# Normalized tiles and heads transposed by DMA, the first slab of keys used by four head pairs, the queries of block 1 computed within block 0

## The chip, the cores and the metric

The kernel runs as one program on the 8 cores of one Trainium2 chip. Each core works on its own data and exchanges nothing with the others. The metric is the device time of the slowest core in microseconds (us), one launch of the kernel; a time is the median of several runs. The kernel before takes 1018.23 us (three runs, 1016.39 to 1018.49).

## The reference

One transformer layer in float32, over x of shape (4, 4096, 1024): multi-query attention (16 heads of 64, one key and one value head) and a small per-channel network, both behind a layer norm and with a residual.

```python
r = layernorm(x)                                   # over the last axis, eps 1e-5
q = einsum('bnd,hkd->bnhk', r, query_proj)         # 16 heads of 64
k = einsum('bmd,dk->bmk', r, key_proj)             # one key head
v = einsum('bmd,dv->bmv', r, value_proj)           # one value head
attn = softmax(einsum('bnhk,bmk->bnhm', q, k) / 8)
o = einsum('bnhm,bmv->bnhv', attn, v)
x = x + einsum('bnhv,dhv->bnd', o, output_proj)
r = layernorm(x)
s = r @ Win + bin_                                 # (b, t, 64)
g = einsum('btmh,mh->btm', relu(s[..., None] * W1 + b1), W2) + b2
x = x + g @ Wout + bout
```

## The kernel before

Two cores share a batch entry: each owns 2048 of its 4096 rows as queries and needs the keys and values of all 4096. A core therefore normalizes 32 tiles of 128 rows (`NTILES`), its own 16 first, then the 16 of its neighbour. Four tiles are a slab of 512 rows, so there are 8 slabs (`NSLAB`).

**The main loop.** The queries are taken in 4 blocks of 512 (`NK`), the 16 heads in 8 pairs (`NHP`). One step of the loop, called an exp below, is one pair, one block of queries and one chunk of 128 keys: TensorE makes the scores of both heads, two matmuls of 512 columns (L662), into one of two PSUM buffers (`spa`, `spb`); ScalarE takes the exponential of 128x1024 values and writes bf16 (`ptu`, L816); TensorE multiplies them with the values in 8 matmuls of 65 columns (L457), the 65th column giving the softmax's sum. There are 4 x 8 x 32 = 1024 of them, numbered 0 to 1023. TensorE issues the scores of exp g+2 when exp g is done, so ScalarE has at most two ahead of it. Each engine works through its instructions in order.

**Segments.** `SEGS` lists in which order pairs and key chunks go. Blocks 1 to 3 take a pair through all 32 chunks, then the next pair. Block 0 has to start before all keys exist: pairs 0 and 1 take slab 0 (exps 0 to 7), then both take slab 1 (exps 8 to 15), pairs 2 to 7 take slabs 0 and 1 (to exp 63), and then each of the slabs 2 to 7 goes through all pairs, 32 exps each, the partial sums being added up in `oacc` (`o_out`, L725). So slab 1 is wanted from exp 8, slab 2 from exp 64, slab 3 from exp 96, slab 7 from exp 224.

**Side work.** All else on TensorE is a list of uses (`USES`) that go in turn through two further PSUM banks, `sda` and `sdb`; VectorE empties each (one `sev` count per use, waited for by `wait_ev`). In block 0 (`phase_a_order`) a slab takes four uses `tr` (a normalized tile `r1u` of 128x1024 transposed in 8 matmuls against the identity, L372, and copied out into `r1t` by VectorE, L504), one `K` (8 matmuls of 512 columns, L380) and one `V` (32 of 64 columns, L391). `Q` makes the queries of one pair, 8 matmuls (L402). Of a finished pair the head outputs `on` are transposed in the use `ot` (4 matmuls, L410, copy L517) into `ot`. In blocks 1 to 3 (`later_order`) the output projection of the block before (`op`, two uses a tile), the transposed normalized output tile (`rt`), the small network (`s2`, 23 VectorE operations, `fo`) and queries of a later block are woven in. VectorE also does the layer norm: two `bn_stats` and an aggregation (L468 to L471), then, when GpSimd has made the reciprocal deviation (L836, L838), the normalization (L478).

**The planner.** `pace` runs through the exps in order, without times: when a use is wanted it forces all that stands before it, and otherwise it hands out one piece of TensorE's side work and one of VectorE's an exp. Its counts fix where in each engine's program a piece stands.

**DMA.** SyncE's queue (SP) loads the tiles of x: the first four at once, tiles 4 to 7 into `xtra`, each of the others when the buffer it takes is free (L883, it waits for a normalized tile). GpSimd's queue (POOL) loads the weights, which are converted from float32 to bf16 on the way: `wqb` in eight parts (L854), and `winb`, `woutb` and the output projection `wp`, behind tile 20's deviation (L857 to L860).

The first slab is built by a stretch of its own at the program's start, and the last two output tiles in a tail behind the last exp.

## Time and profile before

| | |
|---|---|
| median of 3 runs | 1018.23 us |
| profiled execution | 1017.6 us |
| its span on the slowest core (core 4) | 1016.1 us (all cores 1012.9 to 1016.1) |
| ScalarE busy | 952.2 us, 94% |
| TensorE busy | 900.6 us, 89% |
| VectorE busy | 358.7 us, 35% |
| chain that ended last | ScalarE's exponential 80% of the span, issue 9%, PE 5%, VectorE 3%, DMA 3% |
| first exp starts, last exp starts | 24.18 us, 984.56 us |

The span runs from the first to the last instruction of a core; the execution's own time is 1.5 us longer. Busy time is the union of an engine's instructions, and exps overlap each other by some 0.3 us, so an exp's own duration is longer than the step from one to the next. A time with "idle before" in a row is what the engine stood still in front of that instruction, and the name behind the arrow is what it then got.

### The profile page before, as it was taken

How to read it: one execution, taken by the hardware profiler on the slowest of the kernel's cores; microseconds unless marked ns; L12 is line 12 of the kernel's file. 1: busy time of each engine (PE TensorE's matmuls, PEld its weight loads, DVE VectorE, ACT ScalarE, POOL GpSimd, SP SyncE). 2: the span in 40 equal slices, each digit the busy share in tenths (PEclk: the TensorE clock that was granted, in tenths of full speed). 3: DMA queues.
4: the chain of work that ended last, by engine and by line, in shares of the span. 5: the costliest groups of instructions: out<-in, count | busy, mean ns of one | idle time of the engine just before them, and what ended most of it. 6: DMA issues, size and time to landing. Idle time of an engine off the chain costs nothing.

```text
span 1016.1 us, 28595 instructions; the slowest of 8 cores (1012.9 to 1016.1 us)
## 1 busy us (share of the span) xinstructions
PE 900.6 (89%) x11582; PEld 493.1 (49%) x11712; DVE 358.7 (35%) x637; ACT 952.2 (94%) x1043; POOL 56.5 (6%) x131
## 2 busy tenths in 40 slices
PE   3898899998899999998889999998889998898884
PEld 3445555555444545544444454544444554454442
DVE  4535666652512222234202122244202326424215
ACT  2597999999999999999999999999999999999981
POOL 3201111100000000000000000000000000000000
PEclk9999999999999999999999999999999999999995
DMA  8502257220000000002200000001210000400101
GB/s 196 138 12 85 85 119 174 85 85 3 1 2 2 2 2 2 2 2 84 85 2 2 1 3 1 2 2 62 58 51 2 2 2 2 167 2 1 44 2 41
DMA packets 13406, 40.94 MB, mean 40 GB/s; under 512 B 3168, under 2 KB 3296, under 8 KB 13152
## 3 DMA queue, kind: packets, MB, share of 16 engines
q1 hardware_dynamic: 8208, 26.26, 8.5%
q0 software_dynamic: 4784, 12.32, 5.3%
q8 instruction: 97, 1.59, 0.7%
q10 hardware_dynamic: 288, 0.52, 0.1%
q14 instruction: 29, 0.24, 0.1%
HBM read 35.70 MB, written 8.39 MB: 43 GB/s over the span
## 4 chain that ended last, share of the span: by engine, by line
ACT 80%; issue 9%; PE 5%; DVE 3%; DMA 3%; POOL 0%; DVEq 0%; SPq 0%; POOLq 0%; ACTq 0%
ACT ptu L816 80%; DMA xtra<-x_own 2%; PE ob L457 1%; DMA xbuf<-x_own 1%; PE spa L662 1%; PE spb L662 1%; DVE r1u L478 1%; PE sda L380 0%; DVE r1t L504 0%; DVE lnst L468 0%; PE spb L695 0%; DVE lnst L469 0%; DVE gacc L787 0%; POOL rstd L838 0%; PE sdb L391 0%
## 5 line engine op out<-in xcount | busy, mean ns | idle before, releaser
L816 ACT ACTIVATE ptu<-spa 128x1024 bf16<-128x1024 f32 x512 | 594.5, 1161 | 17.7 <-PE spa L662 17.6
L816 ACT ACTIVATE ptu<-spb 128x1024 bf16<-128x1024 f32 x512 | 595.9, 1164 | 2.9 <-PE spb L662 2.9
L457 PE MATMUL ob<-vab,ptu 128*128 128x65 bf16 x8192 | 409.1, 195 | 0.7 <-ACT ptu L816 0.5
L457 PEld LDWEIGHTS ob<-vab,ptu 128*128 128x128 bf16 x8192 | 298.4, 97 | 208.4 <-issue 208.4
L662 PE MATMUL spb<-qt,k2t 64*128 64x512 bf16 x1024 | 200.8, 380 | 40.5 <-ACT ptu L816 34.9
L662 PE MATMUL spa<-qt,k2t 64*128 64x512 bf16 x1024 | 200.9, 380 | 36.5 <-ACT ptu L816 28.3
L662 PEld LDWEIGHTS spb<-qt,k2t 64*128 64x128 bf16 x1024 | 63.4, 92 | 127.2 <-issue 108.1
L662 PEld LDWEIGHTS spa<-qt,k2t 64*128 64x128 bf16 x1024 | 62.6, 92 | 114.5 <-issue 95.1
L725 DVE TENSOR_TENSOR oacc<-oacc,ob 128x520 f32<-128x520 f32 x50 | 34.8, 696 | 77.3 <-PE ob L457 77.2
L836 POOL TENSOR_SCALAR lnve<-lnmv 128x1 f32<-128x1 f32 x48 | 12.7, 264 | 658.0 <-DVE lnmv L471 658.0
L527 DVE TENSOR_TENSOR xbuf<-xbuf,sda 128x512 f32<-128x512 f32 x16 | 11.0, 688 | 93.3 <-PE sda L423 80.0
L527 DVE TENSOR_TENSOR xbuf<-xbuf,sdb 128x512 f32<-128x512 f32 x16 | 11.0, 688 | 89.5 <-PE sdb L423 54.9
L732 DVE RECIPROCAL zrec<-ob 128x8 f32<-128x8 f32 x24 | 5.0, 207 | 100.1 <-PE ob L457 99.8
L478 DVE TENSOR_SCALAR r1u<-xbuf,lnmv,rstd 128x1024 bf16<-128x1024 f32 x44 | 35.6, 810 | 9.1 <-POOL rstd L838 9.1
L423 PE MATMUL sda<-xtra,ot 128*128 128x512 bf16 x98 | 37.0, 379 | 0.0
L402 PE MATMUL sdb<-r1t,wqb 128*128 128x512 bf16 x104 | 35.9, 380 | 0.1
L423 PE MATMUL sdb<-xtra,ot 128*128 128x512 bf16 x96 | 35.4, 379 | 0.2 <-issue 0.2
L513 DVE CAST qt<-sdb 128x512 bf16<-128x512 f32 x16 | 11.0, 690 | 69.5 <-PE sdb L402 40.8
L402 PE MATMUL sda<-r1t,wqb 128*128 128x512 bf16 x96 | 34.4, 380 | 0.1
L468 DVE BATCH_NORM_STATS2 lnst<-xbuf 128x6 f32<-128x512 f32 x44 | 30.3, 689 | 10.9 <-DMA xbuf<-x_own 7.7
L513 DVE CAST qt<-sda 128x512 bf16<-128x512 f32 x15 | 10.3, 690 | 61.4 <-PE sda L402 42.9
L469 DVE BATCH_NORM_STATS2 lnst<-xbuf 128x6 f32<-128x512 f32 x44 | 29.7, 676 | 0.0
(123 smaller groups left out, 471.1 us busy)
## 6 DMA issues: line engine op xcount, KB each, us to landing
xbuf<-x_own SPq DMA_DIRECT2D x28, 512.0 KB, 4.4
xbuf<-x_oth SPq DMA_DIRECT2D x16, 512.0 KB, 3.9
out<-xbuf POOLq DMA_DIRECT2D x14, 512.0 KB, 3.6
wqb<-wq POOLq DMA_DIRECT2D x8, 256.0 KB, 9.6
xtra<-x_own SPq DMA_DIRECT2D x4, 512.0 KB, 6.9
xtra<-wp POOLq DMA_DIRECT2D x1, 2048.0 KB, 21.0
boutbc_s<-boutbc SPq DMA_DIRECT2D x1, 512.0 KB, 12.7
out<-xbuf SPq DMA_DIRECT2D x2, 256.0 KB, 2.6
```

The lines of the kernel that those rows point to most:

```text
L402: r = te.matmul(bank[:], wqb[:, b, j, :], r1t[:, a, j, :], start=(j == 0), stop=(j == DCH - 1))
L423: r = te.matmul(bank[:], ot[:, blk % 2, c, t * 128:(t + 1) * 128], wpb[:, c, b * 512:(b + 1) * 512], start=(c == 0), stop=(c == heads - 1))
L457: r = te.matmul(osum[:, hd, c * 65:(c + 1) * 65], ptu[:, g % NPT, hd * 512 + c * 128:hd * 512 + (c + 1) * 128], vab[:, a + i, :], start=(i ...
L468: v.bn_stats(lnst[:, q, 0:6], xt(li)[:, 0:512])
L469: v.bn_stats(lnst[:, q, 6:12], xt(li)[:, 512:1024]).then_inc(bns, 1)
L478: v.tensor_scalar(r1u[:, li % 2, :], xt(li), lnmv[:, q, 0:1], rstd[:, q, :], op0=ALU.subtract, op1=ALU.mult).then_inc(nrm, 1)
L513: v.tensor_copy(qt[:, a % 2, b, :], bank[:]).then_inc(sev, 1)
L527: v.tensor_tensor(xh, xh, bank[:], op=ALU.add).then_inc(sev, 1)
L662: mm = te.matmul(sps[g % 2][:, hh * 512:(hh + 1) * 512], k2t[rows, mc * 128:(mc + 1) * 128], q, start=True, stop=True)
L725: v.tensor_tensor(oacc[:, hp], oacc[:, hp], osum, op=ALU.add).then_inc(oev, 1)
L816: sc.activation(ptu[:, g % NPT, :], sps[g % 2][:], AF.Exp, scale=0.125).then_inc(ex, 1)
L836: e.tensor_scalar(lnve[:, q, :], lnmv[:, q, 1:2], EPS, None, op0=ALU.add).then_inc(veps, 1)
```

## The change

- `SEGS`: pairs 0 to 3 take slab 0 (exps 0 to 15), then slab 1 (16 to 31); pairs 4 to 7 take both (to exp 63). Slabs 2 to 7 are wanted when they were.
- A normalized tile goes from `r1u` to `r1t` by one DMA transpose from SP's queue (`tile_transpose`), without TensorE, PSUM and VectorE. `r1u` has four buffers in place of two; the normalization of tile n waits for the transpose of tile n-4. The same holds for the output tiles (`rt`), except the last two, and for the heads (`head_transpose`, 31 of 32; in the last block two DMAs a pair). The uses `tr`, `rt` and all `ot` but the last are gone.
- `phase_a_order`: V of slab 0 now stands ahead of the first scores; queries of pairs 1 to 3 come before K of slab 1. The queries of block 1 all follow the last V in block 0; those of block k+1 are spread over block k.
- The planner has costs (in hundredths of a us: an exp 92, a matmul of side work 22), a lag that each engine may carry, and puts a transpose at 6 exps from the normalization (`TR_LAG`). It also writes down the order of the transposes for SP (`moves`).
- VectorE may normalize a whole slab ahead of its K (a table `AHEAD`), in block 0 about a tile every 4 exps, from tile 8 at exp 19 to tile 31 at exp 114.
- SP: a tile's transpose is preceded by the load of tile n+4. The transposes of slabs 5, 6 and 7 wait until V of the slab two before has left PSUM, because they take its buffer in `r1t`. Loads of the output tiles 4 to 15 go to POOL's queue. Parts of `wqb` are issued in another rhythm (two behind tile 3).

```diff
-SEGS = [(0, 0, 0, 4), (0, 1, 0, 4), (0, 0, 4, 8), (0, 1, 4, 8)]
-SEGS += [(0, hp, 0, 8) for hp in range(2, NHP)]
+SEGS = [(0, hp, 4 * sl, 4 * sl + 4) for sl in range(2) for hp in range(4)]
+SEGS += [(0, hp, 0, 8) for hp in range(4, NHP)]
...
 def phase_a_order():
-    o = [("V", 0, 0)] + q(0, 1) + slab(1) + [("V", 1, 0)]
-    o += q(0, 2, 3, 4, 5, 6, 7)
+    o = [("V", 0, 0)] + q(0, 1, 2, 3) + [("K", 1, 0), ("V", 1, 0)] + q(0, 4, 5, 6, 7)
     for s in range(2, NSLAB):
-        o += slab(s) + [("V", s, 0)]
-    return o + q(1, 0) + [("ot", 0, hp) for hp in range(NHP - 1)]
+        o += [("K", s, 0), ("V", s, 0)]
+    return o + q(1, *range(NHP))
...
+        pe_lag = min(pe_lag + PIECE * forced, PE_LAG)
+        t = SCORES + HALF * len(halves) + (SWITCH if halves or forced else 0)
+        while head["pe"] is not None and ok(head["pe"], 1):
+            if pe_lag + t + switch + PIECE - SLOT > PE_LAG:
+                break
+            run("pe", pe, "pe")
...
-        r1u = sbuf("r1u", [128, 2, D], BF16)
+        r1u = sbuf("r1u", [128, 4, D], BF16)
...
                 elif kind == "K":
-                    yield [("sev", n)]
-                    wait_ev(te, n - 1)
+                    yield [free, ("trd", 4 * a + 4)]
+                    wait_ev(te, n - 2)
+                    for q in range(4):
+                        te.wait_ge(trl[q], 16 * a)
...
         def ln_norm(v, li):
             v.wait_ge(rsd, li + 1)
-            if 2 <= li < 6:
-                v.wait_ge(ptr, li - 1)
+            if 4 <= li < 8:
+                v.wait_ge(ptr, li - 3)
+            elif li >= 8:
+                v.wait_ge(trl[q], 16 * (li // 4 - 1))
...
-                if 2 <= i <= NHP:
-                    e.dma_start(wqb[:, i - 1], ...).then_inc(wql[i - 1], 16)
+                for c in {2: [1], 3: [2, 3], 5: [4], 6: [5], 7: [6], 8: [7]}.get(i, []):
+                    e.dma_start(wqb[:, c], ...).then_inc(wql[c], 16)
...
+        def tile_transpose(e, li, dst):
+            e.wait_ge(nrm, li + 1)
+            e.dma_start_transpose(dst, r1u[:, li % 4, :]).then_inc(trl[li % 4], 16)
+
+        def head_transpose(e, k, i):
+            n = 8 * k + i
+            if i == 0 and k >= 2:
+                wait_ev(e, USE_NO["op", 4 * (k - 2) + 3, 1])
+            e.wait_ge(onr, n + 1)
+            if k < LAST:
+                e.dma_start_transpose(ot[:, k % 2, i, :]..., on[:, n % 2]...).then_inc(otl[n % 2], 16)
...
+            for kind, n in moves:
...
+                sl = n // 4
+                if n >= 8:
+                    e.wait_ge(nrm, n + 1)
+                    src = xtile(n + 4) if n < NTILES - 4 else xo_r[n % 4]
+                    e.dma_start(xbuf[:, n % 4, :], src).then_inc(xl[n % 4], 16)
+                if sl in (5, 6, 7) and n % 4 == 0:
+                    last = [i for i, u in enumerate(USES) if u[:2] == ("V", sl - 2) or sl == 5 and u[:2] == ("Q", 0)]
+                    wait_ev(e, max(last))
+                tile_transpose(e, n, r1t[:, slab_buf(sl), :, n % 4 * 128:n % 4 * 128 + 128])
...
+                if n == 20:
                     e.dma_start(boutbc[:], bout_d).then_inc(boutl, 16)
```

In the lists below a row is an instruction, or several alike (x8), with its line, what it writes and what it reads. TensorE before, from the first scores to the scores of exp 8 (L662 scores, L457 values, L391 V, L402 Q, L372 a tile's transpose, L380 K):

```order
L662 MATMUL spa<-qt,k2t 128x512 x2
L662 MATMUL spb<-qt,k2t 128x512 x2
L662 MATMUL spa<-qt,k2t 128x512 x2
L391 MATMUL sda<-wvb,r1t 128x64 x32
L402 MATMUL sdb<-r1t,wqb 128x512 x8
L662 MATMUL spb<-qt,k2t 128x512 x2
L457 MATMUL ob<-vab,ptu 128x65 x12
L372 MATMUL sda<-identb,r1u 128x128 x8
L662 MATMUL spa<-qt,k2t 128x512 x2
```

And TensorE with the change, from the same point (L706 scores, L498 values, L426 V, L438 Q):

```order
L426 MATMUL sda<-wvb,r1t 128x64 x32
L706 MATMUL spa<-qt,k2t 128x512 x2
L706 MATMUL spb<-qt,k2t 128x512 x2
L706 MATMUL spa<-qt,k2t 128x512 x2
L438 MATMUL sdb<-r1t,wqb 128x512 x3
L706 MATMUL spb<-qt,k2t 128x512 x2
L498 MATMUL ob<-vab,ptu 128x65 x12
L438 MATMUL sdb<-r1t,wqb 128x512 x5
L706 MATMUL spa<-qt,k2t 128x512 x2
```

V of slab 0 has moved in front of the first scores, and the eight matmuls of Q stand on both sides of the scores of exp 3. Q of pairs 2 and 3 follow in the same way before exps 8 and 12. K of slab 1 stands directly in front of the scores of exp 16, with no exp's work among its matmuls:

```order
L706 MATMUL spa<-qt,k2t 128x512 x2
L706 MATMUL spb<-qt,k2t 128x512 x2
L498 MATMUL ob<-vab,ptu 128x65 x12
L415 MATMUL sda<-r1t,wkb 128x512 x8
L706 MATMUL spa<-qt,k2t 128x512 x2
```

The later slabs' K stand spread over 5 to 8 exps: K of slab 2 begins behind the values of exp 45, that of slab 3 behind 59, of slab 4 behind 74, of slab 5 behind 92, of slab 6 behind 110 and of slab 7 behind 121. VectorE empties V of slab 3 among the work of exp 81, V of slab 4 at exp 100 and V of slab 5 at exp 113.

VectorE before, from tile 5's normalization to K of slab 1 (L478 normalization, L504 a transposed tile out of PSUM, L508 K out of PSUM):

```order
L478 TENSOR_SCALAR r1u<-xtra,lnmv,rstd 128x1024
L504 COPY r1t<-sda 128x8x128
L478 TENSOR_SCALAR r1u<-xtra,lnmv,rstd 128x1024
L504 COPY r1t<-sdb 128x8x128
L478 TENSOR_SCALAR r1u<-xtra,lnmv,rstd 128x1024
L504 COPY r1t<-sda 128x8x128
L504 COPY r1t<-sdb 128x8x128
L508 CAST k2t<-sda 128x512
```

VectorE with the change, behind the second emptying of `ob`, around tiles 6 to 8 (L509 to L515 statistics, L528 normalization, L562 Q out of PSUM):

```order
L528 TENSOR_SCALAR r1u<-xtra,lnmv,rstd 128x1024
L509 BN_STATS lnst<-xbuf 128x6
L513 BN_STATS lnst<-xbuf 128x6
L515 BN_AGGR lnmv<-lnst 128x2
L528 TENSOR_SCALAR r1u<-xtra,lnmv,rstd 128x1024
L562 CAST qt<-sdb 128x512
```

The first row normalizes tile 6, the statistics are those of tile 8, the next normalization is tile 7's, and Q of pair 3 is emptied behind it.

SP's queue with the change, tiles 20 to 23 (the third row's wait for `sem_side_evac` is the one for V of slab 3):

```order
L971 DMA xbuf<-x_oth 128x1024 [waits sem_normed]
L926 DMA_TRANSPOSE r1t<-r1u 128x8x128 [waits sem_side_evac,sem_normed]
L983 DMA boutbc_s<-boutbc 128x1024
L971 DMA xbuf<-x_oth 128x1024 [waits sem_normed]
L926 DMA_TRANSPOSE r1t<-r1u 128x8x128 [waits sem_normed]
L971 DMA xbuf<-x_oth 128x1024 [waits sem_normed]
L926 DMA_TRANSPOSE r1t<-r1u 128x8x128 [waits sem_normed]
L971 DMA xbuf<-x_oth 128x1024 [waits sem_normed]
L926 DMA_TRANSPOSE r1t<-r1u 128x8x128 [waits sem_normed]
```

Before, SP's queue held loads alone there; now four transposes and four loads stand behind that one wait. Behind the waits of slabs 6 and 7 stand four transposes and three loads each. The load of `wp` follows tile 20's deviation as before, which is now due at about exp 64.

## Rows read from the trace of the kernel before

**Rows 1.** The page: busy time and span share of ScalarE's two groups.

```profile
L816 ACT ACTIVATE ptu<-spa 128x1024 bf16<-128x1024 f32 x512 | 594.5, 1161 | 17.7 <-PE spa L662 17.6
L816 ACT ACTIVATE ptu<-spb 128x1024 bf16<-128x1024 f32 x512 | 595.9, 1164 | 2.9 <-PE spb L662 2.9
```

**Rows 2.** Timeline of ScalarE: start, duration, then idle time before and releaser.

```profile
24.18 1.02 ACT L816 ACTIVATE ptu<-spa 128x1024 bf16<-128x1024 f32 x1 [0.32 <-PE spa L662]
28.93 1.02 ACT L816 ACTIVATE ptu<-spb 128x1024 bf16<-128x1024 f32 x1 [1.89 <-PE spb L662]
31.43 1.02 ACT L816 ACTIVATE ptu<-spa 128x1024 bf16<-128x1024 f32 x1 [1.48 <-PE spa L662]
41.78 1.02 ACT L816 ACTIVATE ptu<-spa 128x1024 bf16<-128x1024 f32 x1 [6.58 <-PE spa L662]
51.27 1.02 ACT L816 ACTIVATE ptu<-spa 128x1024 bf16<-128x1024 f32 x1 [2.06 <-PE spa L662]
101.67 1.02 ACT L816 ACTIVATE ptu<-spa 128x1024 bf16<-128x1024 f32 x1 [6.29 <-PE spa L662]
105.29 1.02 ACT L816 ACTIVATE ptu<-spb 128x1024 bf16<-128x1024 f32 x1 [0.77 <-PE spb L662]
...
969.89 1.20 ACT L816 ACTIVATE ptu<-spb 128x1024 bf16<-128x1024 f32 x1
970.81 1.20 ACT L816 ACTIVATE ptu<-spa 128x1024 bf16<-128x1024 f32 x1
...
984.56 1.20 ACT L816 ACTIVATE ptu<-spb 128x1024 bf16<-128x1024 f32 x1
```

**Rows 3.** Timeline of TensorE at the start and at K of slab 2.

```profile
23.70 0.39 PE L662 MATMUL spa<-qt,k2t 64*128 64x512 bf16 x2 [0.20 <-DVE qt L756]
25.68 1.11 PE L391 MATMUL sda<-wvb,r1t 128*128 128x64 bf16 x32
38.56 1.67 PE L380 MATMUL sda<-r1t,wkb 128*128 128x512 bf16 x7 [1.16 <-DVE r1t L504]
...
96.98 3.00 PE L380 MATMUL sda<-r1t,wkb 128*128 128x512 bf16 x7 [2.10 <-DVE r1t L504]
```

**Rows 4.** Timeline of VectorE: tile 7's statistics, a normalization, Q's emptying.

```profile
29.91 0.68 DVE L513 CAST qt<-sdb 128x512 bf16<-128x512 f32 x1
30.52 0.68 DVE L468 BATCH_NORM_STATS2 lnst<-xtra 128x6 f32<-128x512 f32 x1
31.12 0.68 DVE L469 BATCH_NORM_STATS2 lnst<-xtra 128x6 f32<-128x512 f32 x1
35.84 0.81 DVE L478 TENSOR_SCALAR r1u<-xtra,lnmv,rstd 128x1024 bf16<-128x1024 f32 x1
```

**Rows 5.** Stretches (24 to 52, 280 to 986): busy time by engine, PEclk, DMA.

```profile
24.00:52.00 28.00, 22.27 (x289) 12.73 (x289) 15.30 (x28) 15.81 (x17) 6.32 (x12) 1.00 0.58 137
280.00:986.00 706.00, 646.87 (x8279) 346.58 (x8385) 194.72 (x351) 705.00 (x768) 18.80 (x42) 1.00 0.07 21
```

**Rows 6.** DMA queue q1: 2.0 to 2.5 us, 105 to 107.2 us; last row q0, 7 to 10.5 us.

```profile
q1 hardware_dynamic: 128, 0.03, 26.4%
q1 hardware_dynamic: 144, 0.52, 72.9%
q0 software_dynamic: 703, 0.09, 39.9%
```

**Rows 7.** DMA issues: KB each, median us from issue to landing.

```profile
xbuf<-x_oth SPq DMA_DIRECT2D x16, 512.0 KB, 3.9
identb<-ident SPq DMA_DIRECT2D x1, 32.0 KB, 2.2
xtra<-wp POOLq DMA_DIRECT2D x1, 2048.0 KB, 21.0
```

**Rows 8.** DMA issues of 150 to 160 us, while `wp` is loaded.

```profile
xbuf<-x_oth SPq DMA_DIRECT2D x1, 512.0 KB, 10.8
```

274 lines of the change are left out of this document (154 added, 120 removed).

## Prediction

> **What bounds the kernel now.** I read the page's groups first, then ScalarE's timeline, then its stretches. The two exponential groups are all that counts: 1024 of them, each a step of 970.81 - 969.89 = 0.92 us (0.917 over a long row of them) [rows 1, 2]. From 280 to 986 us ScalarE is busy 705.0 of 706.0 us with 768 of them [rows 5]: nothing that TensorE or VectorE save there can shorten the time. The first starts at 24.18, the last at 984.56 [rows 2]. 1023 steps of 0.917 are 938.1, the stretch is 960.4, so 22.3 us at most can be won inside, and the page puts 17.7 + 2.9 = 20.6 us of idle time on TensorE's scores [rows 1]. The timeline names them: 1.89, 1.48, 6.58 and 2.06 before exp 16, then 6.29 and 0.77 at slab 2 [rows 2]; 19.1 of the 20.6. In front of the program stand 24 us, behind it a tail of 31 us that the change leaves alone. So the sum is made at five places, all in front of exp 130.
>
> **Part by part.**
>
> *V of slab 0 before the first scores.* V takes 1.11 us; the first scores stood at 23.70 behind Q's emptying, with 0.20 idle [rows 3]. I take 0.9 us later: the first exp at 25.1.
>
> *Exps 0 to 16.* Before, exp 16 started at 51.27, 12.4 us behind an unbroken row from 24.18 (38.85) [rows 2]. Slab 1 is now wanted at exp 16, not 8, but Q of pairs 1, 2 and 3 at exps 4, 8 and 12. Exp 4: Q's last matmul ends at about 29.2, but VectorE first has two tiles' statistics (four times 0.68 and two aggregations, 3.0) and a normalization (0.81) [rows 4], so Q leaves PSUM at 30.0 and exp 4 starts at 30.5, 1.7 behind a row from 25.1. Exp 8: Q's end 34.3, emptying 0.7 to 0.8, scores 0.5: 35.6, 1.4 lost. Exp 12: Q stands behind the statistics of tile 8 and the normalization of tile 7, which ends at 40.3: 41.3, 2.0 lost. Exp 16: K of slab 1 starts when the scores of exp 15 (behind exp 13, which ends at 43.3) and the values of exp 13 are done, 44.2; its eight matmuls are 8/7 of 1.67 = 1.9 [rows 3], the emptying 0.8, the scores 0.5: 47.4. That holds if tile 7's transpose, issued at 40.7, has landed by 44.2.
>
> *What a transpose by DMA costs.* No row shows one. A tile is 1024 pieces of 256 B. Nearest rows: 128 packets of 256 B (the identity) took 26.4% of 16 engines in 0.5 us, 16.5 ns each on one engine, so a tile is 1.06 us of all 16; the small packets of `wk` (128 B written) took 39.9% of 3.5 us for 703, 32 ns each, so 2.0 us [rows 6]. From issue to landing the identity took 2.2 us [rows 7]. Bounds for a tile alone: 2.2 and 4.2 us; behind a load of x that is under way, 1.6 us more (72.9% of 2.2 us) [rows 6]. I take 1.06 us of the queue and 3.3 to landing. The lower bound of what it can do to the time is nothing, since a landing before its K leaves no trace. Tile 7: 40.7 + 3.3 and part of a neighbour = 44 to 45, so I put exp 16 at 48.2: 3.1 us won against 51.27.
>
> *Slab 2.* Before, K of slab 2 waited for transposes and copies, ran at the lower clock (3.00 us against 1.67 for the same seven matmuls) and cost 6.29 + 0.77 [rows 2, 3]. Now tile 11 is normalized at exp 33 and K begins at 45: 12 x 0.917 = 11 us for a transpose of 3.3 behind one load (3.9 [rows 7]). 7.1 us won.
>
> *Smaller waits.* 20.6 - 19.1 = 1.5 us of idle time elsewhere. VectorE loses 28 + 14 copies of a tile, TensorE as many transposes: I take 1.0 won.
>
> *Slabs 5, 6, 7: the new wait.* Their transposes wait for V of the slab two before to leave PSUM, and K is placed soon behind: exps 81 to 92, 100 to 110, 113 to 121, that is 10.1, 9.2 and 7.3 us, and each about 0.5 more, since K follows the values. In that time q1 has to move four transposes (4 x 1.06) and four, three and three loads (1.6 each), and the last one's landing adds 2.3 (3.9 - 1.6) [rows 6, 7]: 12.9, 11.3 and 11.3 us. Late by 2.3, 1.6 and 3.5. ScalarE has up to two exps of scores in hand, worth 0.6 us after the next scores' own time: 1.7 + 1.0 + 2.9 = 5.6. Where TensorE waits for a `trl` count, the scores of the next exp stand behind it, and ScalarE waits for these. Ends: 0 (SP's own loads spread before the wait) and, with 2.0 us a transpose, 3.8 more in each, 17. I take 5.6, next to the identity's row.
>
> *Heads and output tiles in blocks 1 to 3.* The head DMA has half a tile; the output projection stands 7 exps (6.4 us) behind the pair's end, of which VectorE takes 2: 4.4 us for about 3. Nothing lost. If it were 4.2 + 1.6, 1.4 us less 0.6 in each of three blocks: 2.4. Loads of output tiles wait on POOL for the stores, far from their use. `r1u`'s wait for the transpose four tiles back stands on VectorE with `oacc`'s emptying behind it, but 16 exps behind it in time except at slabs 5 to 7, where it is the same lateness.
>
> Sum against the profiled execution: 1017.6 - 3.1 - 7.1 - 1.0 + 5.6 = 1012.0. The median of the runs is 0.6 above that execution: 1012.6, which I give as 1012.5.
>
> **The rivals.**
>
> *A, the forecast:* 1008 to 1016.
>
> *B, all of it hidden.* The loads behind the three waits are mostly done before, or transposes take less than their slots; then 1018.2 - 11.2 = 1007, down to 1003 if exps 4 to 16 also lose less (5.1 us are counted there). For: ScalarE has no other stops; against: four loads stand behind one wait in the order of SP's queue.
>
> *C, slower: the transposes of slab 5 behind the load of `wp`.* It is issued about exp 66 and needs 21.0 us, 23 exps, so to exp 89; a load of x issued in its middle took 10.8 us in place of 3.9 [rows 7, 8]. The four transposes and four loads of slab 5 start at exp 82 in the midst of it. The last 7 us of `wp` add up to 6.9; VectorE stops too, since tile 24's normalization waits for tile 20's transpose. Then slab 5 costs 1.7 + 6.9 = 8.6, and a load of tile 24 that comes late (stands before the statistics at exp 78) 1 to 2 more, and with 2.0 us a transpose the other slabs 3.8 each. 1018.2 - 11.2 + 8.6 + 3.9 + 1.5 = 1021, up to 1032; it decides from the point at which the waits sum to 11.2 us. I give 1023. For: the same queue and the 10.8. Against: packets of both queues do alternate, and K of slab 4 is placed before. The Trainium skill, "DMA: Bandwidth & Descriptors" ("Queues, rings and completion order"), says that an engine takes turns between its queues packet by packet; by that the 7 us of `wp` would cost slab 5 about half, 3.5, and C's 1021 would be an estimated 1018. The 10.8 beside 3.9 [rows 7, 8] speaks for more than half, since the measured load lost 6.9 us to some 9 of `wp`.
>
> *D, the start does not gain.* Tile 7's transpose stands behind the loads of tiles 8 to 11 and weights (58% DMA share from 24 to 52 us [rows 5]) and lands at 47 or later: exp 16 at 51, 1015.5 with the rest as in A, 1018 with part of C.
>
> *E, a transpose is far dearer.* If its eight blocks of 128x128 went one behind the other, each like the identity's 2.2 us [rows 7], a tile took 17.6 us, 28 tiles 493; the last would land at 30 + 493 = 523 us, wanted at exp 222, 229 us: some 290 us slower, 1310. The Trainium skill, "VectorE: DVE Perf Modes", speaks against the change: "Transpose 128×128: use TensorE if PSUM dest is OK" ("Rules for kernel authors"), with 1309 ns for one block by DMA ("The three transpose paths"). By that, in series, a tile would be 10.5 us and the time an estimated 1110; nothing in this trace shows it.
>
> **How the numbers follow.** Of no change this kernel's measurement can tell 0.2%, 2 us: 1016.2 to 1020.3 is "same". Chances: A 0.37, B 0.22, C 0.25, D 0.12, E 0.04. Faster: A, B and a quarter of D lie under 1016.2, less what of A spills over: 0.60. Same: three quarters of D and the lower edge of C: 0.13. Slower: the rest of C, and E: 0.27. The range leaves out E and the outer parts of B and C: 1003 to 1030; the forecast's own is 1008 to 1016.
>
> **What would show it.** First exp at 25 us; exp 16 at 47 to 49; no idle time at slab 2; waits of ScalarE's exponential at exps 93 to 97, 111 and 122, the first the longest if C holds, with TensorE waiting for a DMA `r1t<-r1u`. A DMA row of about 3.3 us for `r1t<-r1u`. From exp 130 on, no idle time, and a tail of 31 us. Wrong would be: transposes over 6 us to landing, stops in blocks 1 to 3 at the output projection, or an exp step above 0.917.

## The result, and the profile after

The changed kernel takes 1071.95 us (median of 4 runs, 1070.02 to 1106.12) against 1018.05 of the kernel before; the ratio is 1.0526, 95% interval 1.0498 to 1.0554. It is slower by 54 us, and the prediction of 1012.5 (1003 to 1030) was wrong.

The page of the changed kernel (slowest core: 5): queues, the two groups of exponentials (busy us, mean ns, then idle us before them and what ended most of it), K's matmuls, the first half of a tile's statistics, and two DMA issues (count, KB, median us to landing).

```profile
q1 hardware_dynamic: 67920, 35.06, 16.7%
q0 software_dynamic: 6512, 18.61, 6.8%
...
L864 ACT ACTIVATE ptu<-spa 128x1024 bf16<-128x1024 f32 x512 | 557.7, 1089 | 49.5 <-PE spa L706 48.0
L864 ACT ACTIVATE ptu<-spb 128x1024 bf16<-128x1024 f32 x512 | 557.8, 1089 | 16.3 <-PE spb L706 16.0
...
L415 PE MATMUL sda<-r1t,wkb 128*128 128x512 bf16 x56 | 22.6, 465 | 27.7 <-DMA r1t<-r1u 27.6
L509 DVE BATCH_NORM_STATS2 lnst<-xbuf 128x6 f32<-128x512 f32 x44 | 30.4, 690 | 37.0 <-DMA xbuf<-x_oth 27.9
...
xtra<-wp POOLq DMA_DIRECT2D x1, 2048.0 KB, 20.4
r1t<-r1u SPq DMA_TRANSPOSE x42, 5.2
```

ScalarE's idle time went from 17.7 + 2.9 [rows 1] to 49.5 + 16.3 us, and two new waits stand behind it: TensorE's K matmuls for the transposes of tiles, 27.6 us, and VectorE's statistics for loads of x, 27.9 us. A transpose of a tile took 5.2 us from issue to landing, in the median of all 42. ScalarE's timeline on the slowest core (start, duration, then idle time and releaser) shows where the time went:

```profile
23.67 1.02 ACT L864 ACTIVATE ptu<-spa 128x1024 bf16<-128x1024 f32 x1 [1.49 <-PE spa L706]
29.40 1.02 ACT L864 ACTIVATE ptu<-spa 128x1024 bf16<-128x1024 f32 x1 [1.96 <-PE spa L706]
34.95 1.02 ACT L864 ACTIVATE ptu<-spa 128x1024 bf16<-128x1024 f32 x1 [1.76 <-PE spa L706]
41.15 1.02 ACT L864 ACTIVATE ptu<-spa 128x1024 bf16<-128x1024 f32 x1 [2.41 <-PE spa L706]
61.20 1.02 ACT L864 ACTIVATE ptu<-spa 128x1024 bf16<-128x1024 f32 x1 [16.23 <-PE spa L706]
...
130.40 1.02 ACT L864 ACTIVATE ptu<-spb 128x1024 bf16<-128x1024 f32 x1 [11.15 <-PE spb L706]
149.79 1.02 ACT L864 ACTIVATE ptu<-spa 128x1024 bf16<-128x1024 f32 x1 [7.09 <-PE spa L706]
175.05 1.02 ACT L864 ACTIVATE ptu<-spa 128x1024 bf16<-128x1024 f32 x1 [6.05 <-PE spa L706]
198.84 1.02 ACT L864 ACTIVATE ptu<-spa 128x1024 bf16<-128x1024 f32 x1 [6.59 <-PE spa L706]
...
1037.79 1.09 ACT L864 ACTIVATE ptu<-spb 128x1024 bf16<-128x1024 f32 x1
```

These are exps 0, 4, 8, 12 and 16, then 77, 88, 108, 124 and the last, 1023; the last began at 984.56 before [rows 2]. Slab 2's 6.29 us have gone; 16.23 (K of slab 1), 11.15 (K of slab 4), 7.09, 6.05 (both `oacc`) and 6.59 us (K of slab 7) have come.

Why the transposes of slab 1 and tile 19 of slab 4 were late is in the queue that issues them, SP's (start, us that the issue took):

```profile
27.62 23.71 SPq L926 DMA_TRANSPOSE r1t<-r1u  x4
...
104.68 1.36 SPq L926 DMA_TRANSPOSE r1t<-r1u  x1
108.75 0.33 SPq L971 DMA_DIRECT2D xbuf<-x_oth  x1
109.17 10.52 SPq L926 DMA_TRANSPOSE r1t<-r1u  x1
119.78 5.23 SPq L971 DMA_DIRECT2D xbuf<-x_oth  x1
```

A single issue took 1.36 us behind one load of x (1.22 in the later blocks, where nothing stood beside it), about 6 in slab 1, beside parts of `wqb` and loads of x, and 10.52 beside the load of `wp`. So SP itself was blocked, and the load behind the transpose could go out only at 119.78. Landings in three stretches of this core, 23 to 56, 107 to 130 and 200 to 1000 us:

```profile
xbuf<-x_own SPq DMA_DIRECT2D x3, 512.0 KB, 12.5
wqb<-wq POOLq DMA_DIRECT2D x4, 256.0 KB, 14.2
r1t<-r1u SPq DMA_TRANSPOSE x4, 16.7
...
r1t<-r1u SPq DMA_TRANSPOSE x1, 19.9
...
ot<-on SPq DMA_TRANSPOSE x36, 2.3
r1t<-r1u SPq DMA_TRANSPOSE x14, 3.1
```

A tile's transpose takes 3.1 us to land when it is alone, 16.7 beside weights and loads of x, 19.9 beside `wp`. Behind one load of x, with no weights under way (tiles 8 to 18), it took 4.8 to 6.9 us on this core.

For the comparisons below I took each core's exp starts from its timeline in the profiled execution, and the median over the eight cores: us of the first exp, of the stretches between exps, and of the last exp, beside the timed median.

| kernel | first | 0-16 | 16-64 | 64-96 | 96-128 | 128-256 | 256-1023 | last | time | ratio, interval |
|---|---|---|---|---|---|---|---|---|---|---|
| before | 24.0 | 27.1 | 48.9 | 30.1 | 29.3 | 118.0 | 705.3 | 983.9 | 1018.1 | |
| after | 24.8 | 32.9 | 44.9 | 52.0 | 46.1 | 118.3 | 714.4 | 1033.5 | 1072.0 | 1.0526, 1.0498-1.0554 |
| e1 wp late | 25.0 | 33.2 | 44.9 | 38.2 | 57.7 | 118.3 | 714.5 | 1032.4 | 1074.3 | 1.0529, 1.0494-1.0564 |
| e2 wq late | 24.7 | 25.0 | 44.9 | 54.0 | 45.6 | 118.3 | 715.0 | 1027.9 | 1064.9 | 1.0441, 1.0413-1.0470 |
| e3 loads first | 25.3 | 35.7 | 44.9 | 47.0 | 38.0 | 118.3 | 714.3 | 1021.6 | 1062.9 | 1.0418, 1.0387-1.0449 |
| e4 fill | 24.8 | 34.0 | 45.9 | 52.4 | 45.0 | 124.3 | 723.9 | 1052.1 | 1088.3 | 1.0683, 1.0642-1.0724 |
| e5 tiles on TensorE | 24.4 | 25.6 | 46.7 | 30.3 | 31.0 | 118.8 | 713.1 | 991.5 | 1026.5 | 1.0081, 1.0065-1.0097 |
| e6 all three moves | 24.2 | 25.0 | 44.9 | 32.6 | 40.5 | 118.4 | 714.7 | 999.5 | 1036.3 | 1.0174, 1.0142-1.0206 |
| e7 segments alone | 23.8 | 25.7 | 52.6 | 30.1 | 29.3 | 118.9 | 705.4 | 986.7 | 1021.6 | 1.0023, 1.0013-1.0034 |
| e8 half fill | 24.6 | 34.5 | 44.9 | 53.9 | 45.1 | 119.7 | 711.3 | 1034.3 | 1071.2 | 1.0520, 1.0504-1.0537 |
| e9 one piece | 24.9 | 35.3 | 45.3 | 53.3 | 45.1 | 117.5 | 707.6 | 1029.4 | 1066.9 | 1.0481, 1.0467-1.0495 |
| e10 = e5 + e9 | 24.7 | 25.7 | 46.7 | 30.3 | 31.0 | 117.5 | 708.0 | 983.6 | 1019.6 | 1.0015, 1.0005-1.0024 |
| e11 = e10 + e8 | 24.4 | 25.7 | 46.7 | 30.3 | 31.2 | 117.5 | 704.6 | 981.4 | 1016.8 | 0.9986, 0.9968-1.0004 |
| e12 wp in pieces | 24.6 | 33.7 | 45.7 | 53.1 | 44.8 | 118.3 | 714.6 | 1034.8 | 1073.8 | 1.0564, 1.0535-1.0593 |
| e13 = e11, slabs 2, 3 by DMA | 24.7 | 25.6 | 44.9 | 29.8 | 32.1 | 117.4 | 704.8 | 979.6 | 1015.1 | 0.9973, 0.9960-0.9986 |
| e14 = e6 + e9 + e8 | 24.9 | 25.2 | 44.9 | 32.2 | 38.2 | 117.5 | 704.8 | 987.3 | 1024.2 | 1.0064, 1.0051-1.0076 |

Of the change's 50 us on the last exp, exps 0 to 16 hold 5.8, 64 to 96 21.9, 96 to 128 16.8 and 256 to 1023 9.1; exps 16 to 64 give back 4.0. On the slowest core the start is worse still (37.5 on core 5; 27.2 to 37.5 among the eight). The times count one slow execution (the cores of one die at a lower clock) of the changed kernel, e1, e3, e10 and e11 and three of e7, whose medians are 1070.4, 1072.4, 1061.9, 1019.5, 1016.6 and 1021.0 us without them; the ratios leave them out everywhere.

### The profile page after: what moved, and what is told of

Read it like the earlier page. It is cut to its first block, busy times and chain, and to the rows that moved or that the text cites. A ratio compares the mean times of both kernels' runs of the same rounds, so it can differ in the third digit from the quotient of the medians.

```text
span 1068.5 us, 27827 instructions; the slowest of 8 cores (1059.5 to 1068.5 us)
## 1 busy us (share of the span) xinstructions
PE 903.8 (85%) x11252; PEld 466.5 (44%) x11252; DVE 323.0 (30%) x566; ACT 961.7 (90%) x1043; POOL 69.7 (7%) x143
## 3 DMA queue, kind: packets, MB, share of 16 engines
q1 hardware_dynamic: 67920, 35.06, 16.7%
## 4 chain that ended last, share of the span: by engine, by line
ACT 71%; issue 10%; PE 8%; DMA 6%; SPq 3%; DVE 2%; DVEq 0%; POOL 0%; ACTq 0%; POOLq 0%
ACT ptu L864 71%; DMA r1t<-r1u 3%; PE ob L498 3%; SPq L926 2%; PE spa L706 1%; PE spb L706 1%; PE sda L415 1%; DMA xbuf<-x_oth 1%; DMA wvb<-wv 1%; DMA xbuf<-x_own 0%; DVE lnst L509 0%; DVE r1u L528 0%; PE spb L740 0%; PE spa L740 0%; DVE lnst L513 0%
## 5 line engine op out<-in xcount | busy, mean ns | idle before, releaser
L864 ACT ACTIVATE ptu<-spa 128x1024 bf16<-128x1024 f32 x512 | 557.7, 1089 | 49.5 <-PE spa L706 48.0
L864 ACT ACTIVATE ptu<-spb 128x1024 bf16<-128x1024 f32 x512 | 557.8, 1089 | 16.3 <-PE spb L706 16.0
L498 PE MATMUL ob<-vab,ptu 128*128 128x65 bf16 x8192 | 418.3, 197 | 15.0 <-DVE oacc L770 12.7
L498 PEld LDWEIGHTS ob<-vab,ptu 128*128 128x128 bf16 x8192 | 306.6, 99 | 228.8 <-issue 228.8
L706 PE MATMUL spa<-qt,k2t 64*128 64x512 bf16 x1024 | 204.1, 390 | 48.7 <-ACT ptu L864 41.0
L706 PE MATMUL spb<-qt,k2t 64*128 64x512 bf16 x1024 | 204.1, 390 | 47.3 <-ACT ptu L864 44.2
L706 PEld LDWEIGHTS spb<-qt,k2t 64*128 64x128 bf16 x1024 | 56.7, 93 | 147.2 <-issue 138.4
L706 PEld LDWEIGHTS spa<-qt,k2t 64*128 64x128 bf16 x1024 | 56.6, 93 | 142.4 <-issue 135.0
L884 POOL TENSOR_SCALAR lnve<-lnmv 128x1 f32<-128x1 f32 x48 | 17.7, 369 | 793.7 <-DVE lnmv L515 793.7
L415 PE MATMUL sda<-r1t,wkb 128*128 128x512 bf16 x56 | 22.6, 465 | 27.7 <-DMA r1t<-r1u 27.6
L461 PE MATMUL sdb<-xtra,ot 128*128 128x512 bf16 x124 | 43.6, 379 | 0.0
L438 PE MATMUL sdb<-r1t,wqb 128*128 128x512 bf16 x128 | 43.0, 380 | 0.0
L509 DVE BATCH_NORM_STATS2 lnst<-xbuf 128x6 f32<-128x512 f32 x44 | 30.4, 690 | 37.0 <-DMA xbuf<-x_oth 27.9
L438 PE MATMUL sda<-r1t,wqb 128*128 128x512 bf16 x120 | 40.6, 380 | 0.0
L528 DVE TENSOR_SCALAR r1u<-xbuf,lnmv,rstd 128x1024 bf16<-128x1024 f32 x44 | 35.7, 810 | 15.5 <-POOL rstd L886 15.2
L513 DVE BATCH_NORM_STATS2 lnst<-xbuf 128x6 f32<-128x512 f32 x44 | 29.8, 676 | 0.0
L886 POOL TENSOR_TENSOR rstd<-lnve,mhalf 128x1 f32<-128x1 f32 x48 | 27.6, 574 | 7.1
```

What stands on the lines that cost most here:

```text
L415: r = te.matmul(bank[:], wkb[:, j, :], r1t[:, slab_buf(a), j, :], start=(j == 0), stop=(j == DCH - 1))
L438: r = te.matmul(bank[:], wqb[:, b, j, :], r1t[:, a, j, :], start=(j == 0), stop=(j == DCH - 1))
L461: r = te.matmul(bank[:], ot[:, blk % 2, c, t * 128:(t + 1) * 128], wpb[:, c, b * 512:(b + 1) * 512], start=(c == 0), stop=(c == heads - 1))
L498: r = te.matmul(osum[:, hd, c * 65:(c + 1) * 65], ptu[:, g % NPT, hd * 512 + c * 128:hd * 512 + (c + 1) * 128], vab[:, a + i, :], start=(i ...
L509: v.bn_stats(lnst[:, q, 0:6], xt(li)[:, 0:512])
L513: v.bn_stats(lnst[:, q, 6:12], xt(li)[:, 512:1024]).then_inc(bns, 1)
```

## The experiments

Theory after the two traces: a transpose by DMA is cheap alone and very dear beside another queue's transfers, because it is many small packets. Rival: the new order of segments and queries makes the slabs late. A second question is the loss over exps 256 to 1023.

**e1, `wp` loaded at tile 31.**

```
-                if i == 20:
+                if i == NTILES - 1:
```

> GpSimd issues the loads of winb, woutb and wp at tile 31 instead of at tile 20; nothing else changes. Theory T1 (the transposes of slab 4 crawl because the wp load stands beside them on the DMA engines: tile 19's landed 19.87 us after its issue, and exp 77 came 11.25 us late, exps 78 to 80 another 2.1): exp 77's lateness falls under 2 us, the time falls by 11 to 15 us to 1057 to 1061, if the load, now at about 190 us, meets no transpose that something waits for. Exps 88, 108 and 124 stay late by about 6 to 7 each, since SP's own order causes them. Rival R1 (a transpose's own packets are slow, whatever is beside it): tile 19 still lands some 15 to 20 us after its issue and the time stays at 1070 to 1074. Rival R1b: the load, moved to where slab 7's transposes run, makes those late instead: exp 124 is late by over 12 us and the time stays within 4 us of 1072.

Measured: exp 77 is late by 0.8 us at most, and exp 124 by 18.4 us in the median, 27.9 on the slowest core, where 7.0 stood. The slowest core's timeline (SP's issue of one transpose, TensorE's wait), then its DMA landings from 165 to 205 us:

```profile
170.02 22.74 SPq L926 DMA_TRANSPOSE r1t<-r1u  x1
...
202.34 0.58 PE L415 MATMUL sda<-r1t,wkb 128*128 128x512 bf16 x1 [27.38 <-DMA r1t<-r1u]
```

```profile
xtra<-wp POOLq DMA_DIRECT2D x1, 2048.0 KB, 27.3
r1t<-r1u SPq DMA_TRANSPOSE x4, 16.7
```

T1's cause and R1b's outcome both hold: the harm moves with the load. R1 falls.

**e2, three parts of `wqb` behind tile 7's transpose.**

```
+                if i == 8:
+                    e.wait_ge(trl[3], 16)
-                for c in {2: [1], 3: [2, 3], 5: [4], 6: [5], 7: [6], 8: [7]}.get(i, []):
+                for c in {2: [1], 3: [2, 3], 5: [4], 8: [5, 6, 7]}.get(i, []):
```

> Parts 5, 6 and 7 of wqb are loaded only once tile 7's transpose has landed (parts 1 to 4 as before). Theory T2 (slab 1's transposes, 16.7 us to landing each, share the DMA engines with five parts of wqb): with three parts fewer beside them they land in under 10 us, the wait before exp 16 falls from 11.1 us to 3 to 6, and the time to about 1065 to 1068. Rival R2 (they are slow because of the x loads of tiles 8 to 11, 12.5 us each, and because SP needs 6 us to issue one): landing stays at 14 us or more, exp 16 stays 14 to 16 us late, the time stays at 1070 to 1074. Rival R2b: parts 5 to 7, later, make heads 5 to 7 wait for their queries after exp 40: a new wait of 2 us or more there.

Measured: exp 16 is late by 3.6 us (2.9 to 4.5) in place of 11.7 (6.1 to 16.3); some 7 us of the time. Landings from 23 to 56 us on core 0:

```profile
wqb<-wq POOLq DMA_DIRECT2D x4, 256.0 KB, 6.6
r1t<-r1u SPq DMA_TRANSPOSE x4, 7.1
```

T2 holds, R2 and R2b fall: there is no new wait at heads 5 to 7. On the same core of the changed kernel the two medians are 12.0 and 15.4 us: taking three parts of 256 KB away made both kinds of transfer about twice as fast. The turns that e12 below shows do not account for all of it. The queues of the changed kernel over 33 to 55 us, while the four transposes move:

```profile
q1 hardware_dynamic: 4332, 1.47, 81.7%
q0 software_dynamic: 569, 1.03, 50.0%
```

For each packet of the weights 7.6 of q1 went through, and one of them took 66 ns in the mean (81.7% of 16 engines' 22 us for 4332), where a tile alone needs 21 (40.4% of 3.4 us for 1056). That the parts of `wqb` do it is shown by the edit; by what means is not.

**e3, the x loads of slabs 5 to 7 ahead of the wait.**

```
-                if n >= 8:
-                    e.wait_ge(nrm, n + 1)
+                loads = [n] if 8 <= n < 20 else range(n, n + 4) if n >= 20 and n % 4 == 0 else []
+                for m in loads:
+                    e.wait_ge(nrm, m + 1)
```

> In slabs 5, 6 and 7, SP issues the four x loads of the next slab before it waits for the slab's buffer and issues the four transposes; before, each load stood between two transposes, behind the wait. Theory T3 (exps 88 and 108 are late because VectorE waits 8.80 and 6.82 us for an x load that stood behind SP's wait for V, and TensorE then waits for oacc): both VectorE waits go below 2 us, exps 88 and 108 are late by under 2 us, the time falls by 8 to 13 us to 1059 to 1064. Rival R3 (the loads only take the transposes' place: four loads of 3 to 4 us and four transposes share the same engines, so the transposes land later by what the loads gain): exps 108 and 124 are late by 8 us or more from TensorE's wait for r1t, and the time stays within 4 us of 1072.

Measured: exp 88 not late at all (7.0 before the edit), 108 by 2.3 (6.0), 124 by 3.2 (7.0), and 0.6 new at 92; some 9 us of the time. VectorE in the changed kernel, then in e3, where the wait has become one for a transpose that frees `r1u`:

```profile
146.89 0.69 DVE L509 BATCH_NORM_STATS2 lnst<-xbuf 128x6 f32<-128x512 f32 x1 [8.80 <-DMA xbuf<-x_oth]
170.47 0.69 DVE L509 BATCH_NORM_STATS2 lnst<-xbuf 128x6 f32<-128x512 f32 x1 [6.82 <-DMA xbuf<-x_oth]
```

```profile
164.94 0.81 DVE L528 TENSOR_SCALAR r1u<-xbuf,lnmv,rstd 128x1024 bf16<-128x1024 f32 x1 [3.90 <-DMA r1t<-r1u]
```

T3 holds, but for exp 108, which was to be late by under 2 us: two of the stops came from the order of SP's queue, through VectorE, which has `oacc` behind the statistics. R3 falls.

**e6, the three moves together** (`wp` once tile 31's transpose has landed).

```
+                if i == NTILES - 1:
+                    e.wait_ge(trl[3], 16 * 7)
```

> The changed kernel with three moves of DMA issues, all transposes still by DMA: winb, woutb and wp are loaded only once tile 31's transpose has landed, parts 5 to 7 of wqb only once tile 7's has, and in slabs 5 to 7 SP issues the four x loads ahead of the wait and the transposes. Theory T6 (each late exp is a transpose or an x load that stands beside or behind another DMA, so the repairs add up): exp 16 late by about 4 us (as with the second move alone), exp 77 by under 2, exp 88 by under 2, exps 108 and 124 by 2 to 4 each; the time is 1072 less 12, 13, 7, 3 and 3, 1030 to 1038. Rival R6 (the load of wp goes on to disturb what comes after, the transposes of heads and the first output projection at exp 263, or the gains do not add up): the time is over 1045.

Measured: 1036.3, exp 16 late by 3.2, 77 and 88 by nothing, 92, 108 and 124 by 1.7, 2.9 and 4.6. T6 holds but for exp 124, which was to be late by 4 at most: the moves add up (1030 to 1038 were expected), and `wp` disturbs nothing behind. Exps 96 to 128 still take 40.5 in place of 29.3.

**e12, `wp` in eight DMAs.**

```
+                    for c in range(DCH):
+                        e.dma_start(wpb[:, c, :], wp_d[:, c * D:(c + 1) * D]).then_inc(wpl, 16)
```

> The changed kernel with the load of wp cut into 8 DMAs of 128 x 1024 (packets of 4096 bytes by the DMA rows, where the whole one had 16384); bytes and place are unchanged. Theory T12 (the engines take turns between queues packet by packet, so a transpose of 1024 packets of 256 bytes waits for one 16384-byte packet of 1.2 to 1.8 us per turn): with packets a quarter as long tile 19's transpose lands in under 12 us in place of 19.87, exp 77 is late by 3 to 6 us in place of 11.25, the time is 1063 to 1067. Rival R12 (the transposes wait for the load's bytes, or for its writes, and not for its packets): tile 19 still lands only when the load has ended, exp 77 is late by 10 us or more, the time is 1070 to 1074.

Measured: no change; exp 77 late by 12.4 us, and tile 19's transpose landed after 20.6. But the queues (packets, MB, share of 16 engines) over 10 us in the midst of the load, in the changed kernel (114 to 124 us) and in e12 (118 to 128), tell how it happens:

```profile
q0 software_dynamic: 97, 1.51, 89.2%
q1 hardware_dynamic: 90, 0.37, 13.1%
```

```profile
q0 software_dynamic: 835, 1.52, 95.2%
q1 hardware_dynamic: 841, 0.21, 17.7%
```

One packet of q1 for one of q0, whatever their sizes: 90 to 97, and 841 to 835. The packets of `wp` were recorded as 16384 and, in pieces, 2048 bytes, eight times smaller and not four, as I had expected; at 84 turns per us a tile's 1024 packets need 12 us by themselves. In the changed kernel q1's 90 packets were those of the load of x that SP had issued just before tile 19's transpose: 128 packets of 4096 bytes at 9 per us are 14 us, and the transpose came behind them. The landing of that load, issued at 108.75, and the queues from 126 to 129 us:

```profile
xbuf<-x_oth SPq DMA_DIRECT2D x1, 512.0 KB, 19.5
...
q1 hardware_dynamic: 1144, 0.56, 99.3%
q0 software_dynamic: 19, 0.05, 8.1%
```

The load landed at 128.28 and the transpose at 129.04. Its small packets moved only when `wp` was nearly through, and took few turns beside it: what cost the time there was the load of x in front of them. In e12 this load landed after 8.7 us, and it was the transpose's own packets that then took turns with the 2048-byte ones. The issue of the transpose took 2.5 to 4.6 us on the eight cores of e12, where the changed kernel has 9.6 to 11.9, so the edit freed SP but not the transpose. R12's outcome holds, and the turns on which T12 rested exist: T12 failed since it never counted them. The Trainium skill, "DMA: Bandwidth & Descriptors" ("Queues, rings and completion order"), has the rule of turns packet by packet; the two pairs of rows agree with it.

**e5, tiles 4 to 31 of block 0 back on TensorE and VectorE.**

```
-    o = [("V", 0, 0)] + q(0, 1, 2, 3) + [("K", 1, 0), ("V", 1, 0)] + q(0, 4, 5, 6, 7)
+    o = [("V", 0, 0)] + q(0, 1) + tr(4) + q(0, 2) + tr(5, 6) + q(0, 3) + tr(7)
+    o += [("K", 1, 0), ("V", 1, 0)] + q(0, 4, 5, 6, 7)
...
+                    for j in range(DCH):
...
+                        r = te.transpose(view[:, j * 128:(j + 1) * 128],
+                                         r1u[:, a % 4, j * 128:(j + 1) * 128], identb[:])
```

> The changed kernel with one part undone: tiles 4 to 31 of block 0 are transposed by TensorE into a PSUM bank and moved by VectorE again, as in the kernel before (28 tiles, 8 transposes and one copy of about 1.1 us each); the heads and the later blocks' tiles still go by DMA, and the first slab is still used by four head pairs. x loads are issued by SP as tiles are normalized. Theory T5 (45 of the 54 us come from tile transposes by DMA in exps 0 to 128, which land late beside loads): exps 0 to 128 take 137 to 141 us as before or less instead of 181, and the time is 1020 to 1030, about 10 above the kernel before, since the loss of 10 us over exps 128 to 1023 is not of this part. Rival R5 (the new order of segments and of the queries is what makes slabs 1, 4 and 7 late): exps 0 to 128 still take over 160 us and the time stays above 1045.

Measured: 1026.5; exps 0 to 128 take 133.6 us by the table, less than the 135.4 of the kernel before and the 175.9 of the changed one. 45.5 of the 54 us go with the tile transposes by DMA. The edit also takes away what comes with them, SP's wait for V, the loads of x between the transposes and the normalization a slab ahead, so the 45.5 are for all of this together; e1, e2, e3 and e6 divide them. T5 holds, R5 falls: the new segments are not what is late.

**e7, the kernel before with the new segments alone.**

```
-SEGS = [(0, 0, 0, 4), (0, 1, 0, 4), (0, 0, 4, 8), (0, 1, 4, 8)]
-SEGS += [(0, hp, 0, 8) for hp in range(2, NHP)]
+SEGS = [(0, hp, 4 * sl, 4 * sl + 4) for sl in range(2) for hp in range(4)]
+SEGS += [(0, hp, 0, 8) for hp in range(4, NHP)]
```

> The kernel before with one part of the change alone: the first slab of keys is used by four head pairs, and the queries and transposes of slab 1 are ordered for it; everything is transposed by TensorE and VectorE as before. Theory T7 (the start's gain is real but hidden in the changed kernel by slab 1's transposes): exp 16 comes 2 to 4 us earlier than in the kernel before (51.27), slab 2's stall stays, and the time is 1014 to 1017. Rival R7 (the work of slab 1 between exps 4 and 16 costs as much wherever it stands): exp 16 comes within 1 us of 51.27 and the time stays at 1017 to 1020.

Measured: exps 0 to 16 gain 1.4 us (27.1 to 25.7), but slab 2 comes 7.7 us late in place of 5.1, and exps 16 to 64 lose 3.7; the time is 0.2% above before. T7 had put exp 16 2 to 4 us earlier and the time at 1014 to 1017, R7 exp 16 within 1 us; it came 1.8 earlier, at 49.5. Neither side foresaw the loss in exps 16 to 64. The planner of before puts the transposes of slab 2 behind the four queries that now come later, so the start's gain is worth something only with the new planner (46.7 in e5).

**The loss over exps 256 to 1023: e4, e8, e9.** Counted over the planner's table, exps 256 to 1022 have no side work on TensorE in 421 cases (249 before) and two pieces or more in 75 (26 before). TensorE in the changed kernel at one light stretch:

```profile
562.63 0.39 PE L706 MATMUL spb<-qt,k2t 64*128 64x512 bf16 x2 [0.53 <-ACT ptu L864]
563.55 0.39 PE L706 MATMUL spa<-qt,k2t 64*128 64x512 bf16 x2 [0.53 <-ACT ptu L864]
563.88 0.54 PE L498 MATMUL ob<-vab,ptu 128*128 128x65 bf16 x12
564.47 0.50 PE L706 MATMUL spb<-qt,k2t 64*128 64x512 bf16 x2
564.90 0.84 PE L498 MATMUL ob<-vab,ptu 128*128 128x65 bf16 x12
565.67 0.61 PE L706 MATMUL spa<-qt,k2t 64*128 64x512 bf16 x2
```

Behind exps without side work and without values, with 0.53 us of idle TensorE each, the same pair of matmuls goes from 0.39 to 0.61 us: the engine has fallen to its lower level, 1.2 GHz (granted clock 0.50 from 564.7 to 567.7 us, 1.00 from 560 to 564), just as 12 matmuls of values are due per exp in place of 8. This core has seven such places over exps 256 to 1023; they cost about 0.4 us in each of three or so exps.

```
+                    light = g >= 130 and not any(counts[w].get(g, 0) for w in ("pe_s", "pe_v", "pe"))
-                    for hh in range(2):
+                    for hh in ([0, 0, 1] if light else [0, 1]):
```

> From exp 130 on, each exp in which TensorE has no side work gets one of its two score matmuls twice (the same result written again): added work of about 0.2 us in an exp that has 0.5 us of idle TensorE. Theory T4 (over exps 128 to 1023 the kernel loses about 10 us, some 6.7 of it where TensorE's granted clock falls to its lower level after stretches without side work, 7 places with three exps of +0.4 each or so): TensorE no longer goes idle 0.5 us per exp there, those places keep the full clock and the time falls by 5 to 8 us to 1064 to 1067. Rival R4 (the clock falls for another reason, or the loss is in the stretches where two side matmuls stand in one exp): the time stays at 1070 to 1074, or rises by up to 5 us for the added matmuls.

Measured: the time is 16 us worse, yet the clock was held. Stretches of TensorE's load and clock (columns as in [rows 5]), of the changed kernel (first) and e4:

```profile
700.00:800.00 100.00, 80.98 (x1072) 45.89 (x1070) 2.70 (x6) 98.92 (x108) 0.00 (x0) 0.97 0.02 5
```

```profile
700.00:800.00 100.00, 97.07 (x1168) 44.48 (x1166) 9.36 (x17) 99.46 (x107) 3.17 (x6) 1.00 0.13 43
```

PEclk is 1.00 in place of 0.97, and TensorE is busy 97%: it has become the bound, with an exp every 0.93 us. T4's time (1064 to 1067) fails; rival R4 holds on the direction, but had at most 5 us more. On the cause of the clock T4 holds.

e8 repeats half of one matmul only:

```
+                    if light:
+                        te.matmul(sps[g % 2][:, 0:256], k2t[0:64, mc * 128:(mc + 1) * 128], q, start=True, stop=True)
```

> The changed kernel with half of the filling tried before: from exp 130 on, an exp without side work on TensorE gets one score matmul of 256 of its 512 columns twice, ahead of the two. The full one kept the granted clock at 1.00 but made TensorE itself the bound (an exp every 0.93 us in place of 0.917). Theory T8 (a little work is enough to keep the clock, and costs nothing because TensorE is idle 0.5 us per light exp): exps 256 to 1023 take 713 us or less in place of 715.0, by 1.5 to 6 us less, the time is 1066 to 1070. Rival R8 (the half matmul either leaves the clock falling, or costs what it gives back): 714 to 718 us for those exps, the time 1070 or more.

Measured: 711.3 us in place of 714.4 over exps 256 to 1023, but 1.4 more over 128 to 256; the time is the same within the interval. T8 holds for the stretch, not for the time, which it had put at 1066 to 1070.

e9 makes the planner's side work more even:

```
-            if pe_lag + t + switch + PIECE - SLOT > PE_LAG:
+            if pe_lag + t + switch + PIECE - SLOT > (PE_LAG if g < 130 else 6):
```

> The changed kernel with one number of the planner lower from exp 130 on: the lag up to which it puts further side work behind an exp is 6 in place of 25, so that over exps 256 to 1023 two pieces or more stand in 22 exps instead of 75 (26 in the kernel before), and none in 361 instead of 421 (249 before). Theory T9 (most of what exps 256 to 1023 lose, 715.05 us against 705.34, is in the exps with two pieces, which take 0.09 us more, and in what follows them; the light stretches' clock costs 2 to 4): those exps take 709 to 712 us, the time is 1066 to 1069. Rival R9 (all of the loss is the clock of the light stretches): they take 713 to 716 us and the time is 1070 or more.

Measured: 707.6 us, 6.8 of the 9.1 back, and another 0.8 back over exps 128 to 256; the time is 1066.9, as T9 had it. The clock was hardly touched: over exps 256 to 1023 the granted clock is 0.986 to 0.993 on the eight cores, against 0.983 to 0.993 without the edit. So R9 falls, and two pieces in one exp cost more than I had put there (T9 said 709 at best).

**Together: e10 (e5 + e9) and e11 (+ e8 from exp 256).**

> Tiles 4 to 31 of block 0 on TensorE and VectorE again (1026.45 us by itself), with the planner's lag of 6 from exp 130 on. Theory T10 (the two repairs add up): exps 256 to 1023 take 709 to 712 us in place of 716.2, the time is 1019 to 1023, the same as the kernel before (1018.2) or slower by up to 0.5%, since the light stretches' clock still costs 2 to 4 us. Rival R10 (what is left of the loss in exps 256 to 1023 comes from the transposes of heads by DMA and the order of the queries, not from how pieces are packed): 715 us or more, the time over 1024.

> The kernel of the run before this one, and from exp 256 on the half score matmul twice in each exp without side work, which raised the granted clock to 1.00. Theory T11 (clock and packing are two causes of the same loss): exps 256 to 1023 take 705 to 709 us, near the 705.3 of the kernel before, and the time is 1014 to 1018, the first to be at or under the kernel before. Rival R11 (the fill costs what it gives back): within 2 us of the kernel without it.

Measured: 1019.6 and 1016.8. T10 and T11 hold on the time, and the stretches came out a little better than they had put them (709 and 705 at best): 708.0 and 704.6 us over exps 256 to 1023, the latter 0.7 under the kernel before, with all heads but the last and the later tiles by DMA. So these transposes cost the later blocks nothing; the planner's packing and the clock did.

**e13, e11 with slabs 2 and 3 by DMA; e14, the best with all tiles by DMA.**

```
+BY_DMA = range(8, 16)
...
+                if n in BY_DMA:
+                    tile_transpose(e, n, r1t[:, slab_buf(n // 4), :, n % 4 * 128:n % 4 * 128 + 128])
```

> The best kernel so far (tiles 4 to 31 of block 0 on TensorE, planner's lag of 6 from exp 130 on, half fill from exp 256 on: 1016.8 us) with tiles 8 to 15 alone transposed by DMA, as in the changed kernel: slabs 2 and 3, where no load of weights is under way. Theory T13 (slab 2's gain of the prediction is real where nothing stands beside the transposes): exps 16 to 64 take 44.9 us in place of 46.7 and the 1.9 us at exp 64 goes, exps 64 to 128 stay within 1 us of 63.1, the time is 1013 to 1016. Rival R13 (tiles 16 to 31, now planned some ten exps earlier, run into the load of wp or are late from x loads on SP): what exps 16 to 64 gain is lost by exp 128, and the time stays within 1 us of 1016.8.

> All transposes by DMA, with the three moves of DMA issues (1036.3 us by themselves), the planner's lag of 6 from exp 130 on and the half fill from exp 256 on. Theory T14 (what is left is slabs 5 to 7, where one buffer after the other makes four loads and four transposes of SP follow the wait for V): exps 256 to 1023 take 705 us, exps 96 to 128 still about 40 in place of 29.3, and the time is 1025 to 1028, 9 to 11 above the kernel with the tiles on TensorE. Rival R14 (part of the loss over exps 256 to 1023 belongs to the tile transposes after all): 708 us or more there, the time 1030 or more.

Measured: e13 takes 1015.1 us, ratio 0.9973 (0.9960 to 0.9986), the only kernel here that is shown to be faster than the one before. Exps 16 to 64 take 44.9 us, exps 64 to 128 61.9 against 61.5, and the wait at exp 64 is gone (1.9 in e11): T13 holds on both. That e13 is faster than e11 is read from these stretches; the intervals of the two ratios overlap, so by the times alone R13 is not excluded. On its slowest core one transpose of heads met the stores and loads of output tiles. ScalarE's row, and that core's DMA issues from 862 to 876 us:

```profile
874.58 1.02 ACT L903 ACTIVATE ptu<-spa 128x1024 bf16<-128x1024 f32 x1 [3.20 <-PE spa L745]
```

```profile
xbuf<-x_own POOLq DMA_DIRECT2D x4, 512.0 KB, 6.7
out<-xbuf POOLq DMA_DIRECT2D x1, 512.0 KB, 5.9
ot<-on SPq DMA_TRANSPOSE x2, 5.8
```

e14 takes 1024.2, 7.4 us above e11, and 7.0 of that is in exps 96 to 128 (38.2 against 31.2): T14 holds for the place, with a smaller price. R14 falls. In e14 nothing is lost at slab 1 (exps 0 to 16 take 25.2 us, 25.7 in e11) or at exp 77; exps 92, 108 and 124 are late by 1.3, 1.9 and 3.5 us.

## Why the prediction was wrong, step by step

The step that failed is the price of a transpose beside other traffic. The prediction put a tile at "1.06 us of the queue and 3.3 to landing" and 1.6 more behind a load. Alone that was right: 3.1 to landing, 21 ns a packet against 16.5; behind a load of x it was nearly right, 4.8 to 6.9 where 4.9 were put. Beside weights it was 7.1 (e2) to 19.9 us. Two things were missing. The load of x in front of the transpose was priced at 1.6 us more; when it shares the engines with `wp` it takes 19.5, and the transpose lands 0.8 behind it. And where a transpose's own packets share the engines with another queue, each waits a turn: 12 us for a tile in e12. Neither accounts for slab 1, where the small packets were three times slower than alone; there only the cause, the parts of `wqb`, is shown.

- First exp at 25.1: 24.8 in the median; V cost no more than taken.
- Exps 0 to 16: without the collision (e2) exp 4, 8 and 12 are late by 2.1, 1.9 and 2.5 (predicted 1.7, 1.4, 2.0), and the stretch takes 25.0 us, 2.1 less than before, where 23.1 were forecast. In the changed kernel it took 32.9. The condition named there, that tile 7's transpose lands by 44.2, is what broke (it landed at 53.6 us on core 0 and at 55.6 on core 5); rival D had the place, and its 47 was far too early.
- Slab 2, 7.1 won: the place was right, the size 4.0 in the median and 5.5 on the slowest core (50.4 to 44.9). The 7.06 were read on one of the two cores of before that stall longer (6.3 us at exp 64) than the other six (4.8), and over exps 16 to 64 the changed kernel loses 0.9 against an unbroken row.
- Smaller waits, 1.0 won: nothing of it shows. Exps 128 to 256 take 118.3 us, 118.0 before.
- Slabs 5 to 7, 5.6 us: once the loads go first (e3), exps 92, 108 and 124 are late by 0.6, 2.3 and 3.2, 6.1 together. That this is so near the 5.6 is luck in part: with the weights out of the way too (e6) they are late by 1.7, 2.9 and 4.6, 9.2 together. As made, exps 88, 108 and 124 are late by 7.0, 6.0 and 7.0, 20.0 together, and at 88 and 108 the cost came by another way: a load of x behind SP's wait for V, VectorE's statistics behind it, `oacc` behind these. The sum counted what q1 must move, but not who else waits behind SP.
- Rival C had the right cause, the load of `wp`, but said that "K of slab 4 is placed before": K stands before, at exp 74, but tile 19's transpose, which it needs, was issued at 109.17 us, behind the load of `wp` (107.88), at about exp 66 as forecast. The cost was 12.0 us at exp 77 in place of 6.9 at slab 5. Exps 88 and 108 owe nothing to `wp`: in e1 they stay late by 7.2 and 6.1.
- Its argument against, that "packets of both queues do alternate", was true (90 to 97) and pointed the other way: it is why the load of x took 19.5 us. The half price that I had drawn from the Trainium skill's rule of turns holds only between packets of one size.
- Blocks 1 to 3, "Nothing lost": 9.1 us. The heads' landing was right (2.3 us), but the planner's new packing (6.8 us, e9) and the clock of the light stretches (3.4, e10 to e11) were not looked at; that ScalarE is busy 705.0 of 706.0 us [rows 5] says only that nothing can be won there, not that nothing can be lost.
- Rival E: eight blocks in series would have shown 17.6 us for a tile alone; 3.1 exclude it. The advice of the Trainium skill, "VectorE: DVE Perf Modes" ("Rules for kernel authors"), to use TensorE, held for the kernel as made. With the loads moved (e14) it held for slabs 5 to 7, whose transposes wait for a buffer, and not for slabs 1 and, by e13, 2 and 3.

Not settled: why SP's issue of a transpose takes from 1.22 to 22.74 us. It goes with what the engines carry, since smaller packets of the same load shorten it (2.5 to 4.6 us in e12), but no run shows what it waits for. Nor is it settled why the start differs so much among cores, or what slows the packets in slab 1.

## What to carry to other kernels

Count a transfer in packets as well as in bytes, and count what stands in front of it on its own queue: beside `wp` each packet took a turn, so a load of x with 128 packets held up the transpose behind it, and in e12 the transpose's 1024 packets took as many turns. Place it where no load of weights runs, and let such loads wait for its landing. A blocked issue holds everything behind it on its queue; list who waits for those. A stage that is full before has nothing to give but much to lose: compare, before and after, how many steps carry no side work and how many carry two pieces.

## What the runs showed of the hardware

- Beside the load of `wp` DMA queues took turns by packets, whatever their size: 97 to 90 with packets of 16384 against 4096 bytes, 835 to 841 with 2048 against 256. Beside the parts of `wqb` it was not one for one: 569 to 4332.
- Splitting a load into smaller packets did not speed up a transpose beside it, 20.6 us to landing against 19.9, but it did speed up the load of x in front of the transpose, 8.7 against 19.5, and the transpose's issue, 2.5 to 4.6 against 9.6 to 11.9.
- A transpose of 128x1024 bf16 by DMA landed after 3.1 us alone and 4.8 to 6.9 behind one load of 512 KB.
- An issue of a DMA transpose held its queue for 1.22 us alone, 10.52 and 22.74 us beside a large load.
- TensorE fell to the lower of its levels when work was taken off it: 0.39 to 0.61 us for a pair of matmuls behind exps in which it stood idle for 0.53 us. One half matmul more per light exp held the clock at 1.00 and won 3.4 us (e10 to e11).
